# Attention: the second operations of shift and quotient stand behind the next maxima and free the shared PSUM bank themselves

## The chip, the cores and the metric

The kernel runs on one core of one Trainium2 chip. The time is the device time of that core in microseconds (us); several executions are timed, and one more is recorded by the hardware profiler. Engines: PE (TensorE, matmul), PEld (its weight loads, which overlap PE), DVE (VectorE), ACT (ScalarE), POOL (GpSimd), SP (SyncE, which only issues DMAs here).

## What is computed

A stack of eleven steps on x of 16 sequences x 512 tokens x 128 features: attention, recurrent feed-forward, Mamba, feed-forward, latent attention (MLA), mixture of experts, rotary attention, mixture of experts, with layer norms between. The change is in attention, which is used three times with 16 heads of 8 features:

```python
scores = jnp.einsum('bhqd,bhkd->bhqk', q, k) / jnp.sqrt(jnp.float32(D_K))
scores = scores + rel_bias.transpose(2, 0, 1)[None]          # first attention only
scores = jnp.where(causal[None, None], scores, -jnp.inf)     # first and third
attn = jax.nn.softmax(scores, axis=-1)
out = jnp.einsum('bhqk,bhkd->bhqd', attn, v)
out = out.transpose(0, 2, 1, 3).reshape(b, t, d)
return out @ WO.T + bO
```

## The kernel before

`attend` (line 1065) is called three times: with a relative bias and causal (called L0 here), not causal (MLA), and causal with a mask (ROT). A *group* is four heads of one sequence: 4 groups a sequence, 64 groups a call. Each engine has its own hand-written instruction stream, and the streams meet only through semaphores.

The scores are computed twice. `scores_s` (line 1245) puts queries on the partitions, so that DVE (`maxima`, line 1433) can find each query's maximum along the free axis. `scores_t` (line 1272) puts keys on the partitions for exp on ACT (line 1412) and the product with V (`pv`, line 1308, accumulated in `o_ps`). The maxima of a group are turned by PE (`mt`, line 1325), negated and split into a high and a low bf16 part by DVE (`shifts`, line 1465: two operations, the second reads the first's result), stored to DRAM and loaded back by SP as two more rows of the queries (`store_m` line 1182, `load_t` line 1165). The scores run three groups ahead (`AHEAD`).

A group is a step of NTILE tiles for each of two pairs of heads: 3 tiles a pair in the causal calls, numbered 0 to 5 here, 4 a pair, 0 to 7, in MLA. In each tile PE does scores_t of group g, scores_s of group g + 3 and a piece of `pv` of group g - 1. Both kinds of scores go through rings of three PSUM banks (`t_ps`, `s_ps`), two banks a tile, so PE may start scores_s of a tile when DVE has read the second head of the tile before last and the first head of the last tile. In L0 the tiles 0 and 3 get their bias on DVE (`add_bias`, line 1452, line 1460), and the bank of scores_t is free when that is done.

The last PSUM bank, `misc`, is shared by four small uses, in a fixed order; each takes the bank when `misc_read` has counted the use before. They stand behind the tile that `misc_at` names, in PE's stream and in DVE's:

- MT: `mt` on PE, then `shifts` on DVE;
- OT: `ot` on PE (line 1333) turns the group's output, then `divide` on DVE (line 1479) takes the reciprocal of the sums and multiplies;
- BT, once in four groups: `bt` on PE (line 1340), `gather` on DVE (line 1492);
- WO, once in four groups: `wo` on PE (line 1347), `add` on DVE (line 1496) adds the result into x.

In `shifts` and `divide` the second operation follows the first at once behind a wait for it, and a third wait, for the second operation, stands before a sequencer instruction that counts `misc_read` up (lines 1477 and 1490). Inside `maxima` the causal calls count a semaphore `s_seen` before their operations; MLA does not.

Of the kernel before, what the change touches and what calls it, by code (L numbers as in the profile page):

```python
# [25 lines left out]
NB = 16  # L26
# [1038 lines left out]
def attend(core, x, stacks, v_dram, shift_dram, w, scale, causal, bias=None):  # L1065
# [13 lines left out]
    if causal:  # L1079
        tiles = [[(0, 512, 0, 0)], [(0, 384, 1, 128)], [(0, 256, 2, 256), (256, 128, 3, 384)]]  # L1080
        s_tiles = [[(0, 512, 3)], [(0, 128, 0), (128, 384, 2)], [(0, 256, 1)]]
        pv_pieces = [None, (0, 0, 256), (0, 256, 512), (1, 128, 512), (2, 256, 512), (3, 384, 512)]
        misc_at = dict(MT=1, OT=2, WO=4, BT=5)
    else:
        tiles = [[(0, T, k, 0)] for k in range(4)]
        s_tiles = [[(0, T, c)] for c in range(4)]
        pv_pieces = [None, (0, 0, 512)] + [(c, at, at + 256) for c in range(1, 4) for at in (0, 256)]
        misc_at = dict(MT=1, OT=3, WO=5, BT=7)
# [13 lines left out]
    with core.phase() as ph:  # L1102
# [31 lines left out]
        divided = ph.sem("divided")  # L1134
# [18 lines left out]
        def _(sp):  # L1153
# [28 lines left out]
            def store_m(b, k):  # L1182
                bb, g = spread(b, k)
                sp.wait_ge(shift_ready, 2 * (4 * bb + g) + 2)
                sp.dma_start(shift_dram[ds(bb, 1), 4 * g:4 * g + 4].rearrange("a h c r t -> (a h c) r t"),
                             shift[:, g % 2]).then_inc(m_stored[g % 2], 16)
# [6 lines left out]
            store_m(0, 0)  # L1193
            store_m(0, 1)
# [3 lines left out]
            def step(b, g):  # L1198
                n = 4 * b + g
                sp.wait_ge(s_mm, 2 * NTILE * (n + 2) + 2 * NTILE)  # L1200
                load_s(b, g + 4)
                if not (isinstance(b, int) and n == 0):
                    sp.wait_ge(t_mm, USES_OF_GROUP * n)
                sp.wait_ge(v_ready, n + 1 + 1)
                load_t(b, g + 1)
                store_m(b, g + 2)
# [34 lines left out]
        def _(pe):  # L1241
# [98 lines left out]
            def bt(no, b):  # L1340
                use(no)
                pe.wait_ge(divided, 2 * (4 * b + 3) + 2)
# [14 lines left out]
            def step(b, v, g):  # L1357
                started = 4 * b + g if isinstance(b, int) else 99
                for pair, i in itertools.product(range(2), range(NTILE)):
# [11 lines left out]
                    if at == misc_at["BT"] and g == 1 and started >= 4:  # L1371
                        bt(use_no(b, g, "BT"), b - 1)
# [13 lines left out]
            bt(last + 2, NB - 1)  # L1386
# [43 lines left out]
        def _(dve):  # L1430
# [34 lines left out]
            def shifts(no, b, k):  # L1465
# [4 lines left out]
                if not (isinstance(n, int) and n < 2):  # L1470
                    dve.wait_ge(m_stored[g % 2], 16 * (2 * bb + g // 2))
                dve.tensor_scalar(shift[:, g % 2, 0], misc[0:16, 0:P], -1.0, None, ALU.mult).then_inc(shift_ready, 1)
                dve.wait_ge(shift_ready, 2 * n + 1)
                dve.scalar_tensor_tensor(shift[:, g % 2, 1], misc[0:16, 0:P], -1.0, shift[:, g % 2, 0],
                                         ALU.mult, ALU.subtract).then_inc(shift_ready, 1)
                dve.wait_ge(shift_ready, 2 * n + 2)
                dve.sem_inc(misc_read, 1)

            def divide(no, b, k):

                n, g = 4 * b + k, k % 4
# [19 lines left out]
            for k in range(3):  # L1501
                for pair, i in itertools.product(range(2), range(NTILE)):
                    maxima(0, 0, k, pair, i)
                if k:
                    shifts(k - 1, 0, k - 1)

            def step(b, v, g):
                started = 4 * b + g if isinstance(b, int) else 99
                for pair, i in itertools.product(range(2), range(NTILE)):
# [20 lines left out]
            divide(last, NB - 1, 2)  # L1530
            divide(last + 1, NB - 1, 3)
# [835 lines left out]
```

## Time and profile before

| | |
|---|---|
| median of three timed runs | 5572.13 us (5568.46 to 5575.24) |
| profiled execution, own time | 5531.82 us |
| its span | 5529.6 us |
| mean granted TensorE clock | 0.904 |
| busy: PE, DVE, ACT, POOL | 4268.0, 3617.1, 2857.4, 1613.7 us |
| `attend` L0, MLA, ROT in steady flow, us from the span's start | 240 to 1019, 2860 to 3590, 4370 to 4978 |

A busy time is the sum of an engine's operations; semaphore, register and DMA-issuing instructions are not in it. In a row of the timeline the number in brackets at the end is the idle time of that engine just before the instruction, with the one that released it. Small tiles overlap a little, so start to next start is shorter than the duration. The releaser is inferred: where two conditions end close together, the name can be that of either.

### The profile page before, as it was taken

How to read it: one execution, taken by the hardware profiler on the slowest of the kernel's cores; microseconds unless marked ns; L12 is line 12 of the kernel's file. 1: busy time of each engine (PE TensorE's matmuls, PEld its weight loads, DVE VectorE, ACT ScalarE, POOL GpSimd, SP SyncE). 2: the span in 40 equal slices, each digit the busy share in tenths (PEclk: the TensorE clock that was granted, in tenths of full speed). 3: DMA queues.
4: the chain of work that ended last, by engine and by line, in shares of the span. 5: the costliest groups of instructions: out<-in, count | busy, mean ns of one | idle time of the engine just before them, and what ended most of it. 6: DMA issues, size and time to landing. Idle time of an engine off the chain costs nothing. (4 is left out here: it accounts for less than half of the span.)

```text
span 5529.6 us, 110801 instructions
## 1 busy us (share of the span) xinstructions
PE 4268.0 (77%) x31637; PEld 2118.3 (38%) x31638; DVE 3617.1 (65%) x8801; ACT 2857.4 (52%) x5331; POOL 1613.7 (29%) x1559
## 2 busy tenths in 40 slices
PE   6499999987576766778868889853987588885498
PEld 3144444542122222226312222233973233333397
DVE  2488888546699999984279999950115688885012
ACT  7255555664455555556547777731323366663132
POOL 3000000010577777751200000055534100005552
PEclk9699999997799999999669999976998799997699
DMA  7522222003200000000532222213654333331366
GB/s 246 145 76 70 69 75 70 25 22 137 89 25 25 25 25 28 33 13 2 186 96 74 71 77 72 76 52 114 212 176 156 123 92 91 92 90 54 123 212 191
DMA packets 546189, 501.98 MB, mean 91 GB/s; under 512 B 163774, under 2 KB 482911, under 8 KB 545788
## 3 DMA queue, kind: packets, MB, share of 16 engines
q1 hardware_dynamic: 527724, 460.95, 28.0%
q0 software_dynamic: 18160, 37.42, 2.0%
q8 instruction: 135, 2.21, 0.2%
q14 instruction: 170, 1.39, 0.1%
HBM read 330.57 MB, written 167.58 MB: 90 GB/s over the span
## 5 line engine op out<-in xcount | busy, mean ns | idle before, releaser
L1412 ACT ACTIVATE p_probs<-p_t_ps 128x512 f32<-128x512 f32 (+1 forms) x2304 | 1141.8, 551 | 716.6 <-PE p_t_ps L1303 274.8
L1933 PE MATMUL p_y_ps<-p_prod,c_ident 128*128 128x512 f32 x1024 | 550.1, 663 | 307.8 <-DVE p_prod L2116 306.9
L1316 PE MATMUL p_o_ps<-p_probs,p_v_st 128*32 128x256 f32 (+3 forms) x8704 | 726.7, 407 | 2.9 <-ACT p_o_sb L1398 2.9
L2065 POOL TENSOR_TENSOR p_dbx<-p_dtx,p_b_sb 128x512 f32<-128x512 f32 x512 | 642.6, 1279 | 253.2 <-ACT p_b_sb L1964 245.4
L1237 POOL TENSOR_TENSOR p_v_st<-p_v_raw,p_ones 128x128 f32<-128x128 f32 x192 | 87.7, 457 | 2145.8 <-PE p_o_ps L1316 2022.5
L1449 DVE TENSOR_REDUCE p_row_max<-p_s_ps 128x1 f32<-128x512 f32 x1072 | 659.0, 681 | 81.6 <-PE p_s_ps L1254 43.5
L2107 DVE TENSOR_TENSOR_SCAN p_state<-p_da,p_dbx 128x512 f32<-128x512 f32 x512 | 597.7, 1205 | 74.4 <-ACT p_da L2002 54.1
L1285 PE MATMUL p_t_ps<-p_t_q,p_t_k 50*128 50x512 bf16 (+3 forms) x3072 | 516.0, 336 | 164.1 <-ACT p_probs L1412 65.2
L1254 PE MATMUL p_s_ps<-p_s_k,p_s_q 48*128 48x512 bf16 (+3 forms) x3216 | 508.1, 340 | 164.7 <-DMA p_s_k<-stack_k 66.3
L1446 DVE CUSTOM_DVE_ANT_0 p_tried<-p_s_ps,p_s_bias 128x512 bf16<-128x512 f32 (+3 forms) x1072 | 471.5, 487 | 120.2 <-PE p_s_ps L1254 95.8
L1446 DVE CUSTOM_DVE_ANT_0 p_tried<-p_s_ps,c_mask_row 128x512 bf16<-128x512 f32 (+3 forms) x1072 | 469.0, 488 | 104.4 <-PE p_s_ps L1254 49.4
L795 DVE TENSOR_TENSOR p_y<-p_out_ps,p_raw 128x256 f32<-128x256 f32 x142 | 60.3, 424 | 692.7 <-PE p_out_ps L746 692.7
L1933 PEld LDWEIGHTS p_y_ps<-p_prod,c_ident 128*128 128x128 f32 x1024 | 188.7, 202 | 568.0 <-DVE p_prod L2116 489.8
L1285 PEld LDWEIGHTS p_t_ps<-p_t_q,p_t_k 50*128 50x128 bf16 x3072 | 148.9, 93 | 600.8 <-ACT p_probs L1412 343.2
L1964 ACT ACTIVATE p_b_sb<-p_b_ps 128x512 f32<-128x512 f32 x256 | 152.5, 596 | 436.0 <-PE p_b_ps L1902 416.3
L807 POOL DMA_INDIRECT weighed_rows<-p_y,p_raw x284 | 273.2, 962 | 289.3 <-DVE p_y L795 244.8
L2002 ACT ACTIVATE p_da<-p_dt,p_rate 128x512 f32<-128x512 f32 x512 | 334.9, 685 | 29.9 <-DVE p_state L2107 27.9
L777 ACT ACTIVATE p_hidden<-p_hid_ps 128x512 f32<-128x512 f32 x284 | 169.6, 597 | 315.3 <-PE p_hid_ps L735 315.2
L2116 DVE TENSOR_TENSOR p_prod<-p_state,p_c_ps 128x512 f32<-128x512 f32 x512 | 321.7, 668 | 0.0
L1295 PE MATMUL p_t_ps<-p_bias_parts,c_flip 64*128 64x384 bf16 (+2 forms) x4608 | 302.7, 269 | 0.0
L658 POOL DMA_INDIRECT routed_rows<-p_rows,p_index x256 | 252.5, 986 | 121.8 <-issue 73.5
L1412 ACT ACTIVATE p_probs<-p_probs 128x512 f32<-128x512 f32 x256 | 158.4, 628 | 239.2 <-DVE p_probs L1460 239.2
(254 smaller groups left out, 7017.1 us busy)
## 6 DMA issues: line engine op xcount, KB each, us to landing
p_wb<-in_w SPq DMA_DIRECT2D x142, 512.0 KB, 3.7
p_s_q<-stack_q SPq DMA_DIRECT2D x408, 96.0 KB, 2.2
p_s_k<-stack_k SPq DMA_DIRECT2D x408, 96.0 KB, 2.3
p_t_q<-stack_q SPq DMA_DIRECT2D x390, 96.0 KB
p_t_k<-stack_k SPq DMA_DIRECT2D x390, 96.0 KB
mamba_inputs<-p_out SPq DMA_DIRECT2D x17, 1536.0 KB, 5.6
p_inp<-mamba_inputs SPq DMA_DIRECT2D x17, 1536.0 KB, 6.7
stack_q<-p_parts SPq DMA_DIRECT2D x51, 384.0 KB, 2.6
```

Of the source, the lines that this page charges most:

```text
L1254: mm = pe.matmul(s_ps[:, banks[r], at:at + width], s_q[rows, g % 2, pair, c * P:(c + 1) * P], s_k[rows, g % 2, pair, 0:width], start=True, ...
L1285: mm = pe.matmul(out[r], t_k[rows, g % 2, pair, c * P:(c + 1) * P], t_q[rows, g % 2, pair, first:first + width], start=True, stop=not mask ...
L1295: mm = pe.matmul(out[r], bias["flip"][rows, k], bias["t"][q][rows, k, 2 * g + pair, first - c * P:first - c * P + width], start=False, sto ...
L1316: mm = pe.matmul(o_ps[32 * j:32 * j + 32, at:to], v_st[:, g % 2, c, j, :], probs[:, g % 2, j, place[c] + at - first:place[c] + to - first] ...
L1412: act.activation(exps, tile, ACT.Exp, scale=scale).then_inc(expd, 1)
L1446: read = dve.tensor_tensor_reduce(tried[:, slot, at:at + width], scores, over, 1.0, LOWEST, ALU.add, ALU.max, found)
L1449: read = dve.tensor_reduce(found, scores, X, ALU.max)
L1933: pe.matmul(y_ps[:, h], w["ident"], prod[:, k_slot(n, h, RS)], start=(n == 0), stop=(n == STATE - 1)).then_inc(acc_mm, 1)
L2002: act.activation(da[:, k_slot(n, h, RA)], dt[:, u, h], ACT.Exp, scale=rate[:, h, n:n + 1]).then_inc(da_ready, 1)
L2065: pool.tensor_tensor(dbx[:, k_slot(n, h)], dtx[:, u, h], b_sb[:, n % RB], ALU.mult).then_inc(dbx_ready, 1)
L2107: dve.tensor_tensor_scan(out=state[:, out], data0=da[:, k_slot(n, h, RA)], data1=dbx[:, s], initial=0.0, op0=ALU.mult, op1=ALU.add).then_i ...
L2116: dve.tensor_tensor(prod[:, s], state[:, s], c_ps[:, n % 2], ALU.mult).then_inc(prod_ready, 1)
```

## The change

1. `shifts` becomes `shift_high` (behind the maxima of tile MT, as before) and `shift_low` (behind the maxima of the next tile). The low part's operation itself counts `misc_read`; the wait for it and the counting instruction are gone.
2. `divide` is split in the same way: `sums_inverted` behind tile OT, `divide` behind the next one, and the product counts `misc_read`.
3. In the causal calls OT moves from tile 2 to 3 and WO from 4 to 5; in MLA WO moves from 5 to 6. This holds for PE and DVE alike. BT stays.
4. SP's `store_m` waits for `misc_read` of its use, and `bt` drops its own wait for the quotient, since `misc_read` says the same.

```diff
-        misc_at = dict(MT=1, OT=2, WO=4, BT=5)
+        misc_at = dict(MT=1, OT=3, WO=5, BT=5)
...
-        misc_at = dict(MT=1, OT=3, WO=5, BT=7)
+        misc_at = dict(MT=1, OT=3, WO=6, BT=7)
...
-            def store_m(b, k):
+            def store_m(no, b, k):
                 bb, g = spread(b, k)
-                sp.wait_ge(shift_ready, 2 * (4 * bb + g) + 2)
+                sp.wait_ge(misc_read, no + 1)
...
-            def bt(no, b):
+            def bt(no):
                 use(no)
-                pe.wait_ge(divided, 2 * (4 * b + 3) + 2)
...
-            def shifts(no, b, k):
+            def shift_high(no, b, k):
...
                 dve.tensor_scalar(shift[:, g % 2, 0], misc[0:16, 0:P], -1.0, None, ALU.mult).then_inc(shift_ready, 1)
-                dve.wait_ge(shift_ready, 2 * n + 1)
+
+            def shift_low(b, k):
+
+                bb, g = spread(b, k)
+                dve.wait_ge(shift_ready, 4 * bb + g + 1)
                 dve.scalar_tensor_tensor(shift[:, g % 2, 1], misc[0:16, 0:P], -1.0, shift[:, g % 2, 0],
-                                         ALU.mult, ALU.subtract).then_inc(shift_ready, 1)
-                dve.wait_ge(shift_ready, 2 * n + 2)
-                dve.sem_inc(misc_read, 1)
-
-            def divide(no, b, k):
+                                         ALU.mult, ALU.subtract).then_inc(misc_read, 1)
+
+            def sums_inverted(no):
+                dve.wait_ge(misc_mm, no + 1)
+                dve.reciprocal(inv[:, :, :], by_head(misc)[:, :, :, DK]).then_inc(inverted, 1)
+
+            def divide(b, k):
 
                 n, g = 4 * b + k, k % 4
-                view = misc[:, :].rearrange("p (c j d) -> p c j d", c=4, j=4)
-                dve.wait_ge(misc_mm, no + 1)
-                dve.reciprocal(inv[:, :, :], view[:, :, :, DK]).then_inc(divided, 1)
-                dve.wait_ge(divided, 2 * n + 1)
-                dve.tensor_tensor(o_n[:, :, 4 * g:4 * g + 4, :], view[:, :, :, 0:DK],
+                dve.wait_ge(inverted, n + 1)
+                dve.tensor_tensor(o_n[:, :, 4 * g:4 * g + 4, :], by_head(misc)[:, :, :, 0:DK],
                                   inv[:, :, :].unsqueeze(3).to_broadcast([P, 4, 4, DK]), ALU.mult
-                                  ).then_inc(divided, 1)
-                dve.wait_ge(divided, 2 * n + 2)
-                dve.sem_inc(misc_read, 1)
+                                  ).then_inc(misc_read, 1)
...
                     if at == misc_at["MT"]:
-                        shifts(use_no(b, g, "MT"), b, g + 2)
+                        shift_high(use_no(b, g, "MT"), b, g + 2)
+                    if at == misc_at["MT"] + 1:
+                        shift_low(b, g + 2)
                     if at == misc_at["OT"] and started >= 2:
-                        divide(use_no(b, g, "OT"), b, g - 2) if g >= 2 else divide(use_no(b, g, "OT"), b - 1, g + 2)
+                        sums_inverted(use_no(b, g, "OT"))
+                    if at == misc_at["OT"] + 1 and started >= 2:
+                        divide(b, g - 2) if g >= 2 else divide(b - 1, g + 2)
```

## Rows read from the trace of the kernel before

**Rows 1.** Busy time by engine (PE, PEld, DVE, ACT, POOL), clock, DMA: L0, MLA, ROT.

```profile
240.00:1019.00 779.00, 708.64 (x9578) 348.64 (x9578) 690.02 (x2583) 397.94 (x829) 29.36 (x64) 1.00 0.27 72
2860.00:3590.00 730.00, 656.71 (x5732) 190.08 (x5728) 670.41 (x1243) 549.38 (x1031) 27.74 (x61) 0.99 0.27 74
4370.00:4978.00 608.00, 535.79 (x7002) 228.92 (x7000) 526.72 (x2323) 384.14 (x827) 28.74 (x63) 0.99 0.33 91
```

**Rows 2.** Waits of DVE (total us, times, longest) in L0, MLA, ROT.

```profile
DVE p_tried L1446 <- DVE p_shift L1474: 19.6, 52, 0.4
DVE p_probs L1460 <- DVE p_o_n L1486: 13.5, 60, 0.2
...
DVE p_row_max L1449 <- DVE p_shift L1474: 14.7, 57, 0.6
...
DVE p_row_max L1449 <- DVE p_o_n L1486: 13.3, 59, 0.2
...
DVE p_tried L1446 <- DVE p_shift L1474: 25.5, 63, 0.8
DVE p_tried L1446 <- DVE p_o_n L1486: 23.1, 62, 0.4
```

**Rows 3.** Waits of PE, the first row in L0, the second in ROT.

```profile
PE p_t_ps L1285 <- DVE p_probs L1460: 60.3, 127, 0.8
...
PE p_misc L1337 <- DVEq L1477: 21.1, 62, 0.4
```

**Rows 4.** Timeline of one group of ROT: start us, duration us, instruction.

```profile
4597.56 0.69 DVE L1446 CUSTOM_DVE_ANT_0 p_tried<-p_s_ps,c_mask_row 128x512 bf16<-128x512 f32 x1 [0.38 <-PE p_s_ps L1254]
...
4600.29 0.27 DVE L1472 TENSOR_SCALAR p_shift<-p_misc 16x128 bf16<-16x128 f32 x1
...
4600.99 0.66 PE L1337 MATMUL p_misc<-c_ident,p_o_sb 128*128 128x128 f32 x4 [0.32 <-DVEq L1477]
4601.25 0.42 DVE L1446 CUSTOM_DVE_ANT_0 p_tried<-p_s_ps,c_mask_row 128x256 bf16<-128x256 f32 x1 [0.38 <-DVE p_shift L1474]
...
4601.92 0.38 PE L1254 MATMUL p_s_ps<-p_s_k,p_s_q 48*128 48x512 bf16 x2
...
4602.23 0.85 PE L1316 MATMUL p_o_ps<-p_probs,p_v_st 128*32 128x384 f32 x8
4602.23 0.29 DVE L1486 TENSOR_TENSOR p_o_n<-p_misc,p_inv 128x128 f32<-128x128 f32 x1
...
4603.02 0.34 PE L1285 MATMUL p_t_ps<-p_t_q,p_t_k 50*128 50x384 bf16 x2
...
4603.52 0.08 DVE L1446 DVE_READ_ACCUMULATOR2_ANT p_row_max<- 128x1 f32 x1
...
4603.65 0.39 PE L1254 MATMUL p_s_ps<-p_s_k,p_s_q 48*128 48x128 bf16 x4 [0.19 <-DVE p_row_max L1446]
...
4604.24 0.29 DVE L1446 CUSTOM_DVE_ANT_0 p_tried<-p_s_ps,c_mask_row 128x128 bf16<-128x128 f32 x1
...
4605.62 0.42 DVE L1446 CUSTOM_DVE_ANT_0 p_tried<-p_s_ps,c_mask_row 128x256 bf16<-128x256 f32 x1
...
4606.70 0.69 DVE L1446 CUSTOM_DVE_ANT_0 p_tried<-p_s_ps,c_mask_row 128x512 bf16<-128x512 f32 x1 [0.30 <-PE p_s_ps L1254]
```

**Rows 5.** Timeline of L0: bias addition of tile 3, scores_t of tiles 4 and 1.

```profile
612.32 1.29 DVE L1460 TENSOR_TENSOR p_probs<-p_t_ps,xn 128x512 f32<-128x512 f32 x2 [0.22 <-DVE p_o_n L1486]
...
613.07 0.34 PE L1285 MATMUL p_t_ps<-p_t_q,p_t_k 50*128 50x384 bf16 x2 [0.27 <-DVE p_probs L1460]
...
619.40 0.34 PE L1285 MATMUL p_t_ps<-p_t_q,p_t_k 50*128 50x384 bf16 x2 [0.66 <-DVE p_probs L1460]
```

**Rows 6.** Timeline of MLA: scores_s of tile 2, then its maxima.

```profile
3276.46 0.38 PE L1254 MATMUL p_s_ps<-p_s_k,p_s_q 48*128 48x512 bf16 x2
...
3277.18 2.48 DVE L1449 TENSOR_REDUCE p_row_max<-p_s_ps 128x1 f32<-128x512 f32 x4 [0.23 <-DVE p_shift L1474]
```

**Rows 7.** Waits of SP's queue in L0.

```profile
SPq L1162 <- PE p_s_ps L1254: 348.2, 63, 6.7
```

More of the change, by code:

```diff
@@ L1133, in attend @@
         shift_ready = ph.sem("shift_ready")
-        divided = ph.sem("divided")
+        inverted = ph.sem("inverted")
         block = ph.block()
@@ L1192, in _ @@
                 load_s(0, k)
-            store_m(0, 0)
-            store_m(0, 1)
+            store_m(0, 0, 0)
+            store_m(1, 0, 1)
             sp.wait_ge(zeroed, 3)
@@ L1205, in step @@
                 load_t(b, g + 1)
-                store_m(b, g + 2)
+                store_m(use_no(b, g, "MT"), b, g + 2)
             for g in range(4):
@@ L1371, in step @@
                     if at == misc_at["BT"] and g == 1 and started >= 4:
-                        bt(use_no(b, g, "BT"), b - 1)
+                        bt(use_no(b, g, "BT"))
             for g in range(4):
@@ L1385, in _ @@
             ot(last + 1, NB - 1, 3)
-            bt(last + 2, NB - 1)
+            bt(last + 2)
             wo(last + 3)
@@ L1472, in shifts, with by_head @@
                 dve.tensor_scalar(shift[:, g % 2, 0], misc[0:16, 0:P], -1.0, None, ALU.mult).then_inc(shift_ready, 1)
-                dve.wait_ge(shift_ready, 2 * n + 1)
+            def shift_low(b, k):
+                bb, g = spread(b, k)
+                dve.wait_ge(shift_ready, 4 * bb + g + 1)
                 dve.scalar_tensor_tensor(shift[:, g % 2, 1], misc[0:16, 0:P], -1.0, shift[:, g % 2, 0],
-                                         ALU.mult, ALU.subtract).then_inc(shift_ready, 1)
-                dve.wait_ge(shift_ready, 2 * n + 2)
-                dve.sem_inc(misc_read, 1)
-            def divide(no, b, k):
-                n, g = 4 * b + k, k % 4
-                view = misc[:, :].rearrange("p (c j d) -> p c j d", c=4, j=4)
-                dve.wait_ge(misc_mm, no + 1)
-                dve.reciprocal(inv[:, :, :], view[:, :, :, DK]).then_inc(divided, 1)
-                dve.wait_ge(divided, 2 * n + 1)
-                dve.tensor_tensor(o_n[:, :, 4 * g:4 * g + 4, :], view[:, :, :, 0:DK],
+                                         ALU.mult, ALU.subtract).then_inc(misc_read, 1)
[3 more added lines that the diff above has]
+            def divide(b, k):
+                n, g = 4 * b + k, k % 4
+                dve.wait_ge(inverted, n + 1)
+                dve.tensor_tensor(o_n[:, :, 4 * g:4 * g + 4, :], by_head(misc)[:, :, :, 0:DK],
                                   inv[:, :, :].unsqueeze(3).to_broadcast([P, 4, 4, DK]), ALU.mult
-                                  ).then_inc(divided, 1)
-                dve.wait_ge(divided, 2 * n + 2)
-                dve.sem_inc(misc_read, 1)
+                                  ).then_inc(misc_read, 1)
+            def by_head(bank):
+                return bank[:, :].rearrange("p (c j d) -> p c j d", c=4, j=4)
             def gather(no):
@@ L1504, in _ @@
                 if k:
-                    shifts(k - 1, 0, k - 1)
+                    shift_high(k - 1, 0, k - 1)
+                    shift_low(0, k - 1)
             def step(b, v, g):
@@ L1529, in _ @@
             last = use_no(NB, 0, "MT")
-            divide(last, NB - 1, 2)
-            divide(last + 1, NB - 1, 3)
+            for k in (2, 3):
+                sums_inverted(last + k - 2)
+                divide(NB - 1, k)
             gather(last + 2)
```

## The prediction

> **What bounds the kernel now.** The change touches `attend` alone, which runs three times. I read first the busy time of each engine in each attention stage [rows 1]: both PE and DVE are at about 90% in all three (DVE 690 of 779, 670 of 730 and 527 of 608 us; PE 709, 657 and 536), the granted clock is 0.99 to 1.00, and ACT, POOL and the DMA engines have room. So neither engine has a tenth to give; what counts is who waits for whom around the three-bank rings. I call the stages L0 (with the relative bias), MLA (not causal) and ROT (causal with a mask). Each has 16 sequences x 4 groups = 64 groups, so 0.1 us of a group is 6.4 us of the kernel.
>
> Then the waits of DVE in each stage [rows 2]. DVE stands still after its own second shift operation (19.6, 14.7 and 25.5 us) and after its own quotient (13.5, 13.3 and 23.1 us): 109.7 us together, 0.22 us a time where the next step has no counting instruction and nearly 0.4 us where it has one. It is idle that waits for nothing but DVE itself: the operation's completion has to come back before the sequencer may count `misc_read` up and look at the next wait. Last the waits of PE [rows 3]: in L0 60.3 us, twice a group, for `biased` (line 1460), and in ROT 21.1 us, once a group, before the transposes of O (OT, line 1337), for the count at line 1477.
>
> **What the edits do to these waits.** The completion count now comes from the second operation itself, and behind that operation stands no wait on DVE's own work. Between first and second operation a whole maxima tile lies, so that self-wait is satisfied too. The same four operations remain in every group; nothing is added. If all the idle were on the path, 109.7 us would go. It isn't, and I walk one group of each stage to see what is late next.
>
> **ROT** [rows 4]. The group from one tile 0 on DVE to the next is 4597.56 to 4606.70, 9.14 us. With the change, up to the end of the first shift operation nothing differs: 4600.29 + 0.27 + 0.03 - 4597.56 = 3.03. DVE then goes on to tile 2 (before: 0.31 for the second shift operation and 0.38 idle), whose first head takes 0.35 (0.42 less an overlap of 0.07). PE may start scores_s of tile 3 0.13 after that head is read (as 4603.65 follows the head read at 4603.52). From there PE is the late one, since OT now stands behind tile 3's PV piece: scores 0.31 (4601.92 to 4602.23, so 0.07 less than its duration), PV 0.79 (4602.23 to 4603.02), OT 0.59 (0.66 less 0.07), scores_t of tile 4 0.44 (4603.02 to 4603.65, less PE's wait of 0.19), together 2.13. DVE gets tile 4 0.59 after its scores start (4603.65 to 4604.24), takes 1.38 (to 4605.62), then the quotient 0.32 (0.29 at 4602.23 and its gap), then tile 5's first head 0.35, and the next tile 0 comes 0.72 after that (0.13 + 0.59). Sum 3.03 + 0.35 + 0.13 + 2.13 + 0.59 + 1.38 + 0.32 + 0.35 + 0.72 = 9.00 us. So of 0.76 us idle in a group 0.14 us is gained; the rest turns into a wait of DVE for the scores of tile 4: they come 2.13 + 0.59 = 2.72 after those of tile 3 start, while DVE needs 0.59 until it gets tile 3, 1.25 for it and 0.28 for the reciprocal, 2.12, so it stands 0.60. PE's wait of 0.32 before OT (4600.99) goes, as OT comes 1.1 us after the scores of tile 3 while DVE needs 0.35 + 0.28 and a count; it is already in this sum. 64 x 0.14 = **9 us**. Bounds: -0.1 a group (one PE piece 0.3 us longer than I read) to 0.76 (no new wait): -6 to 49 us.
>
> **L0** [rows 5]. PE waits at 613.07 (0.27, scores_t of tile 4, bank held until the bias of tile 3 is added) and at 619.40 (0.66, tile 1). The second one hangs on tile 5's scores, its maxima and then the bias of tile 0: none of that moves, so 0.66 stays. The first one goes: reciprocal, quotient and the idle of 0.22 before the addition at 612.32 now stand behind it or are gone, so the addition comes 0.8 us earlier, and PE, which does the same work in another order, has no pause there. That is 0.27 us, and up to 0.36 if PE's modelled ends hide a little more; I take 0.30. 64 x 0.30 = 19 us. Against it: the addition behind WO now lies between maxima 5 and the bias of the next tile 0, on the path, while before it filled a pause; walked in the same way that costs 0.14 us once in four groups, 2 us. Net **17 us**; bounds 0 (another wait of PE takes the place) to 23.
>
> **MLA** [rows 6]. Scores of tile 2 start at 3276.46 and last 0.38; with 0.04 for the count DVE may read them at 3276.88. DVE ends its first shift operation at 3276.64 (3277.18 less 0.23 idle, 0.28 and 0.03) and would start tile 2 at 3276.88 instead of 3277.18, 0.30 earlier; but the second shift operation, 0.28 and a gap, now follows tile 2: at tile 3 the gain is nil. The shift's idle was hidden by PE's long PV piece ahead of those scores. The quotient's idle is not: before tile 4 the quotient (0.29 + 0.03) and 0.22 idle go, and 0.31 comes back after tile 4. Gain 0.21. 64 x 0.21 = **13 us**; bounds 0 to 0.5 a group (both idles, if the scores of tile 2 come earlier as well), 0 to 32 us.
>
> **The rest, at nothing.** SP: the store of the shifts (line 1185) waits for `misc_read` instead of `shift_ready`, which comes one tile later (0.7 us in the causal stages, 1.2 in MLA). Behind it in SP's queue stands load_s of the next step, and that waits for the scores anyway: 348.2 us in 63 waits in L0, 5.5 each [rows 7]. So the delay is covered; it would take some 5 us to show. BT in a causal stage now follows the quotient of tile 4 closely: PE may wait up to 0.35 us for it once in four groups in ROT, 6 us at most, about made good by WO's move from tile 4 to 5 there; I leave both out. The longer spacing does not touch PE's clock, which is full in all three stages [rows 1]. Prologue and tail: some ten places at 0.1 to 0.3 us, under 3 us, left out.
>
> A rule that speaks against the change: in the trace DVE is idle for 0.22 to 0.38 us behind an operation whose completion it awaits and for about 0.03 us otherwise [rows 2, 4]. The Trainium skill, "VectorE: DVE Perf Modes", section "The DRAIN you can't avoid", says that the pipeline is flushed after each operation whether or not it counts a semaphore, so that counting costs nothing extra, and advises to save operations rather than semaphores. By it the gain would be nothing. It speaks of counting up, though, not of waiting for the count, and the rows of this case differ from it.
>
> **Sum.** 9 + 17 + 13 = 39 us. The profiled execution took 5531.8 us (span 5529.6), so it would take about 5493. The median of the three timed runs is 5572.1, 0.7% above the profiled one; I take the gain off it unscaled: **5533 us**. A measurement of this kernel can tell about 0.2% (11 us) from no change.
>
> **Rivals.** (1) The idle is gained in full: PE keeps up, as it too gets its buffers earlier. For: all 109.7 us are waits for DVE itself, DVE is the busiest engine of MLA. Against: PE is as busy as DVE [rows 1] and has 1.38 us of PV and OT in a row in ROT. It would give 5572 - 105 = about 5467. Chance 0.11. (2) No change within 11 us: what DVE gains, it waits for PE at the next tile, in all three stages; the walk of MLA shows how (0.54 us gone before tile 2, nothing left at tile 3). The rule quoted above, taken as it stands, ends here too: the gap of 0.22 to 0.38 us would remain, behind whatever operation now comes last. 5572. Chance 0.14. (3) Slower: OT behind the long PV piece starves DVE at tile 4. It decides where the scores of tile 4 come more than 0.76 us after DVE is free for them (I get 0.60), or, in L0, where the addition behind WO delays the bias addition. At 0.3 us a group in ROT and 0.15 in L0, 64 x 0.45 = 29 us, less MLA's 13, it gives 5588. For: the only pieces of PE that lie between two scores become 2.13 us where DVE has 1.5 us of work from the moment it gets tile 3. Chance 0.08. The forecast (gains of 15 to 80 us) has 0.67.
>
> **Numbers.** Faster by over 0.2%: 0.67 + 0.11 = 0.78; same 0.14; slower 0.08. The range takes in the forecast case, from 5480 (a gain of 92: most of the three upper bounds 49 + 23 + 32) up to 5576 (no change and its scatter), and leaves out rivals (1) and (3), 0.19.
>
> **What would show it.** In the profile after: no idle on DVE behind the second operations; in its place a wait of DVE for scores before tile 4 in ROT (about 0.6 us a group, 38 us in all) and before tile 2 in MLA (0.24); PE without a wait before OT; PE's wait for `biased` in L0 down from 60.3 to about 43 us; stage lengths shorter by 9 (ROT), 17 (L0) and 13 us (MLA). The prediction is wrong if DVE's idle stays as it is behind the moved operations, if the tile 4 wait exceeds 0.76 us, or if other stages move.

## The result, and the profile after

| kernel | median, us | runs | ratio to before |
|---|---|---|---|
| before | 5570.3 (5556.06 to 5575.24) | 4 | |
| change | 5470.38 (5460.41 to 5478.46) | 4 | 0.983 [0.9803, 0.9857] |

The change is faster by 1.7%. The forecast was 5533 with a range of 5480 to 5576: the direction was right, the size wrong by 63 us, and the range missed the time by 10.

To see where the time came from, I measure each attention stage by one event that both kernels have 64 times: ACT's copy of `o_ps` into `o_sb` (line 1398 before, 1397 after). The rows give the instruction's durations and then the start of its first and its last occurrence; this is ROT, before and then after:

```profile
L1398 ACT ACTIVATE p_o_sb<-p_o_ps x64: 592/592/605, 4388.4 to 4982.2; 128x512 f32<-128x512 f32 x64
```

```profile
L1397 ACT ACTIVATE p_o_sb<-p_o_ps x64: 591/591/603, 4338.5 to 4899.4; 128x512 f32<-128x512 f32 x64
```

| last start less first, us | L0 | MLA | ROT | sum |
|---|---|---|---|---|
| before | 755.7 | 749.9 | 593.8 | 2099.4 |
| after | 736.8 | 720.2 | 560.9 | 2017.9 |
| gained | 18.9 | 29.7 | 32.9 | 81.5 |
| forecast | 17 | 13 | 9 | 39 |

So attention gained 81.5 us: L0 about what was forecast, MLA twice and ROT nearly four times as much. The spans of the two profiles (5529.6 and 5470.2) differ by 59.4 only, because outside attention the profile after took 22 us more. None of it lies in attention, where the change is; the last section says what is known of it.

Busy time by engine (PE, PEld, DVE, ACT, POOL), clock and DMA between those two starts, L0, MLA and ROT, before:

```profile
267.60:1023.30 755.70, 691.21 (x9364) 339.54 (x9360) 669.75 (x2509) 386.63 (x808) 28.00 (x61) 1.00 0.26 71
2855.40:3605.30 749.90, 674.84 (x5912) 196.42 (x5912) 685.23 (x1271) 562.25 (x1056) 27.74 (x61) 0.99 0.27 74
4388.40:4982.20 593.80, 522.49 (x6884) 224.06 (x6884) 513.64 (x2263) 374.63 (x807) 27.83 (x61) 1.00 0.33 91
```

And after:

```profile
265.10:1001.90 736.80, 682.20 (x9364) 348.07 (x9360) 647.42 (x2509) 386.79 (x808) 27.78 (x61) 1.00 0.27 73
2815.00:3535.20 720.20, 666.82 (x5912) 196.41 (x5912) 673.69 (x1271) 562.27 (x1055) 27.74 (x61) 0.99 0.29 77
4338.50:4899.40 560.90, 516.23 (x6884) 227.62 (x6884) 497.50 (x2263) 374.74 (x808) 27.86 (x61) 1.00 0.36 96
```

The windows hold the same instructions (DVE 2509, 1271 and 2263 in both), at the same clock. Yet DVE's *busy* time fell, by 22.3, 11.5 and 16.1 us, 50 together; its idle (length less busy) went from 230.8 to 199.3. In these rows a stretch in which two operations overlap counts once: in ROT the durations alone add up to 637 us before and 633 after, while the busy time is 514 and 498. So 50 us of the 81.5 aren't idle that went, but mostly operations that overlap now and did not before. That is where the size of the forecast failed, and the group below shows it.

The waits changed too. Those of DVE in the steady flow of L0, MLA and ROT (240 to 990, 2825 to 3555, 4300 to 4885; total us, times, longest), where before its own shift and quotient stood [rows 2]:

```profile
DVE p_tried L1445 <- PE p_s_ps L1254: 74.2, 188, 1.1
...
DVE p_row_max L1448 <- PE p_s_ps L1254: 28.2, 67, 4.0
...
DVE p_tried L1445 <- PE p_s_ps L1254: 50.7, 106, 5.7
```

No row of DVE waiting for its own operation is left. In their place DVE waits more for scores: 153 us in all, against 39.0, 14.2 and 20.5 before, 74 together. These windows are not quite those of the table; between the starts of the table, DVE waits 141 us for scores where it waited 68, and 25 us for WO's product (line 1501) where it waited 7. So of 109.7 us of idle some 92 turned into later waits for PE. DVE's idle as a whole fell by 31.5; of that, 14 us are in smaller waits and gaps that I have not taken apart. The wait of PE for the bias in L0 [rows 3], and those of SP's queue in L0 [rows 7]:

```profile
PE p_t_ps L1285 <- DVE p_probs L1459: 52.2, 65, 1.1
...
SPq L1162 <- PE p_s_ps L1254: 252.6, 63, 4.4
SPq L1185 <- DVE p_shift L1477: 86.5, 61, 2.7
```

In L0 PE waits once a group for the bias (65 times) instead of twice (127 times): the wait of `scores_t` of tile 4 is gone. The one of tile 1 grew. Over four groups in a row it was 0.84, 0.65, 0.62 and 0.56 us before (from 509 us on), and is 0.84, 1.03, 0.75 and 0.65 after (from 501 us on). It grew most, by 0.38, where WO's addition now stands in front of the bias addition; there DVE itself waits for WO's product:

```profile
512.03 0.75 DVE L1501 SCALAR_TENSOR_TENSOR x<-p_misc,c_l_b,x 128x512 f32 x1 [0.60 <-PE p_misc L1348]
...
513.44 0.34 PE L1285 MATMUL p_t_ps<-p_t_q,p_t_k 50*128 50x384 bf16 x2 [1.03 <-DVE p_probs L1459]
```

In ROT the wait before OT is gone. There PE waits 0.25 us once in four groups before BT (3.8 us in all), within the 0.35 foreseen, and as much before WO (3.7 us). SP stands 86.5 us for the moved store, and its wait for scores behind it shrinks from 348.2 to 252.6: the delay is covered.

**One group of ROT after**, from one tile 0 on DVE to the next (start us, duration us, instruction, idle ahead and its releaser), to lay beside [rows 4]:

```profile
4527.49 0.69 DVE L1445 CUSTOM_DVE_ANT_0 p_tried<-p_s_ps,c_mask_row 128x512 bf16<-128x512 f32 x1
...
4530.22 0.27 DVE L1471 TENSOR_SCALAR p_shift<-p_misc 16x128 bf16<-16x128 f32 x1
4530.43 0.40 DVE L1445 CUSTOM_DVE_ANT_0 p_tried<-p_s_ps,c_mask_row 128x256 bf16<-128x256 f32 x1
...
4530.89 0.39 PE L1254 MATMUL p_s_ps<-p_s_k,p_s_q 48*128 48x512 bf16 x2
...
4531.99 0.66 PE L1337 MATMUL p_misc<-c_ident,p_o_sb 128*128 128x128 f32 x4
...
4532.59 0.34 PE L1285 MATMUL p_t_ps<-p_t_q,p_t_k 50*128 50x384 bf16 x2
...
4532.87 0.38 PE L1254 MATMUL p_s_ps<-p_s_k,p_s_q 48*128 48x128 bf16 x4
...
4533.45 0.29 DVE L1445 CUSTOM_DVE_ANT_0 p_tried<-p_s_ps,c_mask_row 128x128 bf16<-128x128 f32 x1 [0.49 <-PE p_s_ps L1254]
```

The next tile 0 starts at 4536.10, so the group takes 8.61 us, where it took 9.14 and 9.00 were forecast. The order of events is the one forecast: PE without a pause from scores_s of tile 3 over PV and OT to tile 4, and DVE waiting there, 0.49 us where 0.60 were forecast.

The groups are not all alike. From one `o_sb` to the next ROT takes, over four groups, 9.23, 9.05, 9.79 (with BT) and 10.11 us (with WO) before, and 8.49, 8.45, 9.46 and 9.65 after: 0.74, 0.60, 0.33 and 0.46 less. The forecast's 0.14 was too small in every one of them, and the 0.53 of the group shown is also their mean.

**One group of MLA**, before and then after:

```profile
3265.17 0.28 DVE L1472 TENSOR_SCALAR p_shift<-p_misc 16x128 bf16<-16x128 f32 x1
3265.48 0.28 DVE L1474 SCALAR_TENSOR_TENSOR p_shift<-p_misc,p_shift 16x128 bf16<-16x128 f32 x1
3265.99 2.48 DVE L1449 TENSOR_REDUCE p_row_max<-p_s_ps 128x1 f32<-128x512 f32 x4 [0.22 <-DVE p_shift L1474]
...
3268.39 0.24 DVE L1484 RECIPROCAL p_inv<-p_misc 128x16 f32<-128x16 f32 x1
3268.67 0.29 DVE L1486 TENSOR_TENSOR p_o_n<-p_misc,p_inv 128x128 f32<-128x128 f32 x1
3269.18 7.26 DVE L1449 TENSOR_REDUCE p_row_max<-p_s_ps 128x1 f32<-128x512 f32 x12 [0.22 <-DVE p_o_n L1486]
```

```profile
3208.41 0.28 DVE L1471 TENSOR_SCALAR p_shift<-p_misc 16x128 bf16<-16x128 f32 x1
3208.85 1.29 DVE L1448 TENSOR_REDUCE p_row_max<-p_s_ps 128x1 f32<-128x512 f32 x2 [0.16 <-PE p_s_ps L1254]
3210.06 0.27 DVE L1477 SCALAR_TENSOR_TENSOR p_shift<-p_misc,p_shift 16x128 bf16<-16x128 f32 x1
3210.26 1.26 DVE L1448 TENSOR_REDUCE p_row_max<-p_s_ps 128x1 f32<-128x512 f32 x2
3211.45 0.23 DVE L1482 RECIPROCAL p_inv<-p_misc 128x16 f32<-128x16 f32 x1
3211.73 1.29 DVE L1448 TENSOR_REDUCE p_row_max<-p_s_ps 128x1 f32<-128x512 f32 x2
3212.93 0.28 DVE L1488 TENSOR_TENSOR p_o_n<-p_misc,p_inv 128x128 f32<-128x128 f32 x1
3213.13 6.06 DVE L1448 TENSOR_REDUCE p_row_max<-p_s_ps 128x1 f32<-128x512 f32 x10
```

Read from start to next start, shift and quotient cost DVE 0.82 + 0.79 = 1.61 us a group before, and 0.44 + 0.20 + 0.28 + 0.20 = 1.12 after. The forecast was 1.40.

### The profile page after: what moved, and what is told of

Read it like the earlier page. It is cut to its first block and busy times, and to the rows that moved or that the text cites. A ratio compares the mean times of both kernels' runs of the same rounds, so it can differ in the third digit from the quotient of the medians.

```text
span 5470.2 us, 109878 instructions
## 1 busy us (share of the span) xinstructions
PE 4230.1 (77%) x31637; PEld 2127.4 (39%) x31638; DVE 3565.3 (65%) x8801; ACT 2857.8 (52%) x5331; POOL 1609.7 (29%) x1559
## 5 line engine op out<-in xcount | busy, mean ns | idle before, releaser
L218 PE MATMUL p_var_ps<-p_square,c_mean_mat 128*128 128x512 f32 x256 | 164.1, 727 | 211.6 <-ACT p_square L226 172.8
```

## The experiments

The theory for the size: what was gained comes from DVE's waits for its own operations, and the places do little; my walk undersized it. The rivals: the new places of OT and WO brought the gain, or it is not the wait but the counting instruction that costs. None of the kernels leaves anything out of the computation. "Stages" are lengths as in the table above, L0, MLA, ROT; where a kernel was profiled again they came out within 1 us, MLA within 3.3. The kernel before was profiled once.

| kernel | L0 | MLA | ROT | sum | median, us | before, same chip | ratio |
|---|---|---|---|---|---|---|---|
| change again | 736.8 | 719.9 | 560.7 | 2017.4 | 5422.8 | 5507.1 | 0.9853 [0.9804, 0.9902] |
| count kept | 738.2 | 753.4 | 584.7 | 2076.3 | 5478.54 | 5507.1 | 0.9949 [0.9927, 0.997] |
| count alone | 737.7 | 710.8 | 566.5 | 2015.0 | 5418.26 | 5507.1 | 0.9849 [0.98, 0.9899] |
| places alone | 743.5 | 751.4 | 609.0 | 2103.9 | 5509.66 | 5507.1 | 0.9993 [0.9973, 1.0012] |
| wait kept | 735.4 | 736.6 | 582.2 | 2054.2 | 5455.51, one run | 5507.65 | |
| MT earlier | 724.3 | 711.1 | 565.6 | 2001.0 | 5391.92, one run | 5507.65 | |
| all earlier | 718.3 | 709.9 | 555.8 | 1984.0 | 5380.97, one run | 5507.65 | |
| MLA shift together | 736.8 | 721.3 | 560.8 | 2018.9 | 5426.37 | 5507.65 | 0.9841 [0.9791, 0.9892] |
| early, together | 723.6 | 703.8 | 569.8 | 1997.2 | 5445.69 | 5556.87 | 0.9794 [0.9763, 0.9826] |
| all earlier, timed | 718.5 | 708.1 | 555.9 | 1982.5 | 5428.85 | 5556.87 | 0.976 [0.9727, 0.9794] |
| MLA early, together | 718.3 | 706.8 | 555.8 | 1980.9 | 5443.97 | 5554.6 | 0.9794 [0.9767, 0.982] |
| change, third time | 736.9 | 723.2 | 560.7 | 2020.8 | 5481.4 | 5554.6 | 0.985 [0.9823, 0.9876] |

**The change again**, as made, to stand beside the next three on one chip.

> The change itself, on the chip of the next three kernels. Stage lengths are read from the first to the last move of O (the ACT copy into o_sb) of each attention call: before 755.7, 749.9 and 593.8 us (L0, MLA, ROT), after 736.8, 720.2 and 560.9, so 81.5 us less in attention in one execution each. All theories expect these lengths again within 3 us each. If the 95 us between the medians are attention alone, the lengths must fall by 95; if a stage outside attention scatters (the second routing stage took 21.6 us longer in the one execution of the change), the whole time differs from run to run by more than the attention stages do.

2017.4 against 2017.9: the stages repeat. The median is 84.3 us under the kernel before on the same chip, and attention is 82.0 shorter, so attention accounts for it.

**The count kept.** The moved order, but the second operation is awaited and the sequencer counts, as before.

> The changed kernel with both second operations at their new places, but each followed again by the wait for it and by the sequencer's count of misc_read. Theory A (the gain is DVE's own idle behind the second operations): the idle of 0.22 us (MLA) and nearly 0.4 us (causal) comes back at the new places, twice a group; MLA loses about 0.45 x 64 = 29 us of its 30, ROT and L0 at least 10 each, together 50 to 75 of the 81.5. Rival B (the gain is that PE gets the shared bank sooner and in a better order): only the 0.1 us of the count's way is lost, and attention stays within 15 us of the change. Rival C (the gain is the distance between first and second operation, so that the second one no longer waits): all of it stays.

```diff
-                                         ALU.mult, ALU.subtract).then_inc(misc_read, 1)
+                                         ALU.mult, ALU.subtract).then_inc(second, 1)
+                dve.wait_ge(second, 4 * bb + g + 1)
+                dve.sem_inc(misc_read, 1)
```

(and the same for the product.) It gives back 58.9 of 82 us: 33.5 in MLA, 24.0 in ROT, 1.4 in L0. In sum that is what theory A expects, but not in L0, where at least 10 us should have come back. The idle is back behind the moved operations in MLA:

```profile
3184.50 0.27 DVE L1479 SCALAR_TENSOR_TENSOR p_shift<-p_misc,p_shift 16x128 bf16<-16x128 f32 x1
3185.00 1.29 DVE L1450 TENSOR_REDUCE p_row_max<-p_s_ps 128x1 f32<-128x512 f32 x2 [0.23 <-DVE p_shift L1479]
```

Start to start 0.50 where the change takes 0.20.

**The count alone.** The kernel before in every order and place, but the second operations count `misc_read` themselves; SP's store waits for `misc_read` and BT's own wait is dropped, as in the change.

> The kernel before with one part of the change alone: the second operations count misc_read themselves, nothing stands behind them, and all four operations and OT, WO and BT stay where they were. Theory A: most of the gain is here. MLA 0.45 us a group, 29 us; L0 15 to 20 us; ROT 20 to 33 us; in all 60 to 80 of the 81.5 us. The gap before the second operation, 0.03 us plus the overlap of 0.07 to 0.10 us that neighbours have without a wait, stays lost: 5 to 15 us. Rival C (distance is what counts): less than half, under 40 us. Rival B: PE's wait before OT in ROT shrinks by 0.1 only and the stages gain under 15 us in all.

```diff
                 dve.scalar_tensor_tensor(shift[:, g % 2, 1], misc[0:16, 0:P], -1.0, shift[:, g % 2, 0],
-                                         ALU.mult, ALU.subtract).then_inc(shift_ready, 1)
-                dve.wait_ge(shift_ready, 2 * n + 2)
-                dve.sem_inc(misc_read, 1)
+                                         ALU.mult, ALU.subtract).then_inc(misc_read, 1)
```

84.4 us in attention, as much as the whole change: 2.4 us more in sum, 9.1 better in MLA, 5.8 worse in ROT. Against the kernel before, L0 gains 18.0 and ROT 27.3, both as expected, and MLA 39.1 where 29 were. In MLA both pairs stand together with no idle about them:

```profile
3188.46 0.27 DVE L1471 TENSOR_SCALAR p_shift<-p_misc 16x128 bf16<-16x128 f32 x1
3188.76 0.28 DVE L1473 SCALAR_TENSOR_TENSOR p_shift<-p_misc,p_shift 16x128 bf16<-16x128 f32 x1
3188.98 2.48 DVE L1448 TENSOR_REDUCE p_row_max<-p_s_ps 128x1 f32<-128x512 f32 x4
3191.38 0.25 DVE L1481 RECIPROCAL p_inv<-p_misc 128x16 f32<-128x16 f32 x1
3191.66 0.29 DVE L1483 TENSOR_TENSOR p_o_n<-p_misc,p_inv 128x128 f32<-128x128 f32 x1
3191.87 7.25 DVE L1448 TENSOR_REDUCE p_row_max<-p_s_ps 128x1 f32<-128x512 f32 x12
```

0.52 + 0.49 = 1.01 us a group, against 1.12 in the change and 1.61 before. The second operation, which awaits the first, starts 0.30 and 0.28 us behind it, where one that awaits nothing follows after 0.20: awaiting the operation just issued costs about 0.1 us in this place. So the split into two places was worth nothing in MLA.

**The places alone.** The kernel before with OT at 3 and WO at 5 (6 in MLA).

> The kernel before with OT moved from tile 2 to 3 and WO one tile later, and nothing else: first and second operations together, wait and count as before. Theory A: DVE's idle is all there; MLA unchanged within 2 us, ROT loses PE's wait of 0.32 us before OT but DVE is not faster for it: within 10 us of before; L0 within 10 us. Rival B (the order of PE's work makes the gain): ROT and L0 20 us or more faster.

```diff
-        misc_at = dict(MT=1, OT=2, WO=4, BT=5)
+        misc_at = dict(MT=1, OT=3, WO=5, BT=5)
...
-        misc_at = dict(MT=1, OT=3, WO=5, BT=7)
+        misc_at = dict(MT=1, OT=3, WO=6, BT=7)
```

No gain in sum (4.5 us more in attention, ratio 0.9993): L0 12.2 shorter, ROT 15.2 longer, MLA 1.5 longer. L0 and ROT both moved by more than the 10 us that I had allowed. In ROT the idle behind the shift now delays tile 2, PE stands for its head, and OT behind the late tile 3 delays the next scores, so that both engines stand in turn:

```profile
4567.87 0.42 DVE L1446 CUSTOM_DVE_ANT_0 p_tried<-p_s_ps,c_mask_row 128x256 bf16<-128x256 f32 x1 [0.38 <-DVE p_shift L1474]
...
4568.36 0.39 PE L1254 MATMUL p_s_ps<-p_s_k,p_s_q 48*128 48x512 bf16 x2 [0.64 <-DVE p_row_max L1446]
```

The rival that the places bring the gain falls for the sum, for MLA and for ROT. In L0 it holds in part, and the effects don't add: L0 gains 18.0 by the count alone and 12.2 by the places alone, but 18.9 by both. The traces show that each takes away the same wait. Between the stage's two starts PE waits for the bias 123 times before (58.0 us), and 61 times, once a group, with the count alone (42.9), with the places alone (47.0) and with both (49.9). The wait of `scores_t` of tile 4 is gone in all three.

**The wait kept.** The change, in which DVE waits behind each second operation for its count, with no counting instruction.

> The changed kernel, where each second operation counts misc_read itself, but DVE still waits for that count before it goes on. So PE gets the bank as early as with the change, and DVE has the self-wait but not the sequencer's counting instruction. Theory A (the price is the wait for an own operation): stage lengths close to those with wait and count kept (738.2, 753.4, 584.7), at most 10 us less in all; in MLA at least 740. Rival D (the price is the counting instruction in the sequencer): close to the change (736.8, 719.9, 560.7). Half way, MLA near 735, would mean both.

```diff
                                          ALU.mult, ALU.subtract).then_inc(misc_read, 1)
+                dve.wait_ge(misc_read, no + 1)
```

It gives back 36.8 us: MLA 16.7, ROT 21.5, and L0 1.4 better. In MLA:

```profile
3190.35 0.27 DVE L1477 SCALAR_TENSOR_TENSOR p_shift<-p_misc,p_shift 16x128 bf16<-16x128 f32 x1
3190.74 1.29 DVE L1448 TENSOR_REDUCE p_row_max<-p_s_ps 128x1 f32<-128x512 f32 x2
3191.95 0.25 DVE L1483 RECIPROCAL p_inv<-p_misc 128x16 f32<-128x16 f32 x1
3192.11 1.22 DVE L1448 TENSOR_REDUCE p_row_max<-p_s_ps 128x1 f32<-128x512 f32 x2
```

0.39 us from the start of the second operation to the next tile, against 0.20 without the wait and 0.50 with wait and counting instruction. So in MLA the price has two parts: 0.19 for the wait and 0.11 for the instruction that the sequencer had to issue behind it. The stage says the same (16.7 of 33.5; the expectation had called MLA near 735 the case of both, and it is 736.6). In ROT nearly all that the stage gives back (21.5 of 24.0) is the wait, though DVE's own idle there is 31.8 us with the wait alone and 44.5 with both. Neither cause alone is the answer. In both kernels the reciprocal is 0.16 to 0.17 us ahead of the next tile, where in the change it is 0.28; I don't know why. It gives back 0.12 us a group and is in the stage lengths: 2 x 0.19 - 0.12 = 0.26, times 64 = 17 us, as measured.

**MT one tile earlier**, at 0 in all calls.

> The changed kernel with MT one tile earlier: PE turns the maxima behind tile 0, where no PV piece stands, DVE's first shift operation follows tile 0's maxima and the second one tile 1's. Theory: in ROT and L0 PE waits at tile 1 for ACT or for the bias anyway (28.4 and 52.2 us a stage), so the 0.21 us of this transpose fall into idle time; ROT 5 to 13 us shorter, L0 0 to 10, MLA 5 to 15, as DVE's wait for the scores of tile 2 (0.16 to 0.26 us a group) goes. Rival: PE now waits at MT for the last maxima of the step before (the last head's 0.35 or 0.6 us) and stands there; MLA and ROT 10 us or more longer.

```diff
-        misc_at = dict(MT=1, OT=3, WO=5, BT=5)
+        misc_at = dict(MT=0, OT=3, WO=5, BT=5)
...
-        misc_at = dict(MT=1, OT=3, WO=6, BT=7)
+        misc_at = dict(MT=0, OT=3, WO=6, BT=7)
```

L0 12.5 (0 to 10 expected) and MLA 8.8 us shorter; ROT, which I had expected to be 5 to 13 shorter, 4.9 longer. There PE's wait for ACT nearly went, as expected (27.3 us in the change, 2.9 here), but PE now waits before MT for WO's addition and BT's gather (4.7 and 3.1 us), and DVE waits 58.7 us for scores instead of 40.2. I have not shown which of them makes the stage longer.

**All uses earlier.**

> The changed kernel with every place one earlier: MT 0, OT 2, WO 4, BT 4 in the causal calls and MT 0, OT 2, WO 5, BT 6 in MLA. Against the kernel with MT alone earlier it tells what OT's place is worth once no idle stands behind the operations. Before, moving OT and WO later by one tile cost ROT 15 us and gave L0 12 us. If that comes from PE's order alone, ROT here is about 15 us shorter than with MT alone moved and L0 12 longer. If it came from the idle behind the operations, which stood between the tiles, the two kernels are within 5 us of each other in each stage.

```diff
-        misc_at = dict(MT=1, OT=3, WO=5, BT=5)
+        misc_at = dict(MT=0, OT=2, WO=4, BT=4)
...
-        misc_at = dict(MT=1, OT=3, WO=6, BT=7)
+        misc_at = dict(MT=0, OT=2, WO=5, BT=6)
```

33.4 us below the change in attention: L0 18.5, MLA 10.0, ROT 4.9. Against the run before it, OT's earlier place brought ROT 9.8 (15 expected) and L0 6.0 where I had expected it to cost 12. PE's wait for the bias in L0 shows what was relieved, 23.5 us in 63 waits with MT alone earlier and 25.8 in 63 with all, where the change has 50.4 in 63 (240 to 970 us).

**In MLA the shift together again**, right behind its first operation; the quotient split.

> The changed kernel, but in MLA the two shift operations stand together behind tile 1, the second counting by itself; the quotient stays split, the causal calls as changed. With both pairs together MLA took 710.8 instead of 719.9 us. Theory: the 9 us are DVE's wait for the scores of tile 2 (0.16 to 0.26 us a group), which the second shift operation fills when it stands there; so MLA comes to 711 to 713, L0 and ROT stay at 736.8 and 560.7, attention 9 us below the change, whole time 0.1 to 0.2% below it. Rival: the 9 us come from the quotient together; MLA stays at 718 to 720.

```diff
-                    if at == misc_at["MT"] + 1:
+                    if at == misc_at["MT"] + (1 if causal else 0):
```

I had put down MLA's 9 us to the shift's split alone. It fell: 721.3, no better than the change. The shift now takes 0.52 instead of 0.64 us, but the tile 4 that follows the reciprocal isn't there yet:

```profile
3213.36 0.26 DVE L1471 TENSOR_SCALAR p_shift<-p_misc 16x128 bf16<-16x128 f32 x1
3213.66 0.28 DVE L1477 SCALAR_TENSOR_TENSOR p_shift<-p_misc,p_shift 16x128 bf16<-16x128 f32 x1
3213.88 2.48 DVE L1448 TENSOR_REDUCE p_row_max<-p_s_ps 128x1 f32<-128x512 f32 x4
3216.28 0.25 DVE L1482 RECIPROCAL p_inv<-p_misc 128x16 f32<-128x16 f32 x1
3216.76 1.29 DVE L1448 TENSOR_REDUCE p_row_max<-p_s_ps 128x1 f32<-128x512 f32 x2 [0.23 <-PE p_s_ps L1254]
```

What is gained at the shift is waited for at tile 4. With both pairs together, the quotient's second operation fills that wait (3191.38 to 3191.87 above).

**Early and together.** The count alone, with the places of the version with all uses earlier.

> Both pairs of operations together, the second one counting misc_read itself (no wait and no counting instruction behind it), at the earlier places: MT 0, OT 2, WO 4, BT 4 in the causal calls, MT 0, OT 2, WO 5, BT 6 in MLA. Against the same places with the pairs split (718.3, 709.9, 555.8) it tells what the split itself is worth. Theory: next to nothing, as the split at the old places was worth 0.9 us in L0, 5.8 in ROT (there together with OT's move) and minus 9 in MLA; each stage within 6 us of the split kernel. Rival (the distance between the operations is worth the 0.1 us of overlap twice a group): 12 us longer in each stage.

```diff
-        misc_at = dict(MT=1, OT=2, WO=4, BT=5)
+        misc_at = dict(MT=0, OT=2, WO=4, BT=4)
...
-        misc_at = dict(MT=1, OT=3, WO=5, BT=7)
+        misc_at = dict(MT=0, OT=2, WO=5, BT=6)
```

**All uses earlier, timed**, the same kernel as above, beside it on the same chip.

> The kernel with all places one earlier and the pairs split, again, now timed in rounds. Stage lengths 718, 710 and 556 us again; its whole time 115 us (2.1%) below the kernel before and 33 us (0.6%) below the change, outside the scatter of the other stages.

Together it takes 1997.2, split 1982.5: at these places the split is worth 5.1 us in L0 and 13.9 in ROT, and costs 4.3 in MLA. I had expected a difference within 6 us: right in L0 and MLA, missed in ROT. What the split saves in ROT shows as a wait of PE in the version without it, which the other does not have:

```profile
PE p_s_ps L1254 <- DVE p_row_max L1445: 21.2, 57, 0.4
```

I read it so: the second operation right behind the first delays the head that scores wait for; behind the next maxima it doesn't.

**All uses earlier, in MLA both pairs together**, and **the change a third time**, on one chip.

> The same as the run with every place earlier for the causal heads (second operations behind the next maxima, places one row tile earlier), but in the MLA heads both pairs stand together, each second operation right behind its first, which counts the read. By stages it should be the best of both: L0 718.4, MLA 703.8 (what the run with all pairs together took there), ROT 555.8, sum 1978 us, 4 to 5 us below the run with every place earlier and 39 us below the change as made. Rival: the MLA stage depends on what the stages around it leave behind, and comes out at 708 to 710, so that splitting or not makes no difference there; sum 1983.

> The changed kernel again, to stand on the same chip beside the version with the earliest places: stages 736.8, 720.0, 560.8 and sum 2018, as in its earlier profiles, and 82 us below the kernel before in attention. If the version with the earliest places gains by the stages alone, the two medians differ by 39 us; the rival is that they differ by less than 30 because the stages outside attention take it back.

MLA comes out at 706.8, between the two expectations (703.8 and 708 to 710), and the change's own MLA at 723.2, against 720.2 and 719.9, shows a scatter of 3.3 us; whether the pairs should stand together in MLA stays open. The medians differ by 37.4 us where 39.9 are expected from the stages, so what the earlier places gain, nothing takes back. The best version is the one with all uses earlier, in either form: ratios 0.976 and 0.9794 against the change's 0.985, and on the one chip where both ran, the intervals [0.9767, 0.982] and [0.9823, 0.9876] don't meet.

## Why the prediction was right in direction and wrong in size

**The mechanism held in the main.** Nearly all that was to show did, in its place: no idle on DVE behind its own operations, a wait for scores before tile 4 in ROT (0.49 us, 0.60 forecast) and before tile 2 in MLA (0.16, 0.24 forecast), no wait before OT, PE's wait for the bias in L0 once a group. Its size there is not the forecast one: 52.2 us for 43.

**L0: the number right, in part by luck.** It gained 18.9 for 17. The wait of tile 4 went, as forecast. But "0.66 stays" was wrong: the wait of tile 1 grew by 0.15 us a group, some 9 us in the stage. Most of that is in the group with WO's addition: 0.38 us there, where I had 0.14. So PE's idle fell by 9.9 us, not by 17. The other 9.0 us are busy time of PE that overlaps now. I had allowed 0.03 us a group for that, and it is 0.14. The two errors made up for each other.

**ROT, 0.39 us a group mis-sized.** Measured by the terms of the forecast's sum: up to the end of the first shift operation 2.94 (forecast 3.03); to scores_s of tile 3 0.46 (0.48); from there to scores_s of tile 4 1.98 (2.13); to DVE's tile 4 0.58 (0.59); tile 4 1.38 (1.38); the quotient 0.21 (0.32); the rest 1.06 (1.07). Sum 8.61 against 9.00. The three terms that failed are two kinds:

- The small operations of DVE, "0.27 + 0.03" and "0.32": I took a duration and a gap, as they stand in the row before, where something waits behind them [rows 4]. Without a wait a small operation overlaps its neighbour: 4530.22 to 4530.43 is 0.21 us for an operation of 0.27. That is 0.20 us a group.
- "scores_t of tile 4 0.44 (4603.02 to 4603.65, less PE's wait of 0.19)": without a wait it is 0.28 (4532.59 to 4532.87), so PE had waited 0.35 there, not 0.19. The bracket of a matmul counts from the modelled end of the one before, and that end comes after the next matmul's start even where nothing waits (4532.59 + 0.34 is 4532.93). That is 0.16 us a group.

Both errors have one sign: durations and brackets understate what an engine gains when a wait goes. The 50 us less of busy DVE are the first of them: 0.18 us a group in MLA (11.5 over 64), most of which is the two second operations, each followed after 0.20 us and not after its 0.28, and 0.35 and 0.25 in L0 and ROT, where more operations overlap than I have taken apart.

**MLA, 0.28 us a group.** Of 1.61 us the forecast left 0.51 for the first shift operation, 0.31 for the second, 0.28 for the reciprocal and 0.31 for the product, together 1.41 (1.40 by its gain of 0.21); measured 0.44, 0.20, 0.28 and 0.20. The two operations behind the maxima were priced at 0.31, though nothing waits behind them: 0.22. The remaining 0.07 is tile 2, whose scores came earlier than I read.

Put together: ROT 0.53 us a group times 64 = 34 (stage 32.9), MLA 0.49 times 64 = 31 (29.7), L0 18.9.

**Of the 63 us** between forecast and result, 42.5 are attention's, as above (81.5 less 39). Some 19 more are the part of the 100 us between the two medians that is not attention's, and the change did not make it. With attention's 81.5 alone the time would have been 5489, inside the range. So the sizes were wrong, and it was the part outside attention that put the time below 5480.

**The parts at nothing.** SP's store and the clock were at nothing. BT cost PE 3.8 us of waiting in ROT. WO's move was not the help that I took it for: in ROT PE waits 3.7 us before WO and DVE 9.6 us for its product, and in L0 DVE waits 9.0, where none of these waits stood before. What they cost the stage was not measured.

**The rivals.** (1) All idle gained: fell, though its time of 5467 is next to the measured 5470. That is luck. DVE's idle fell by 31.5 of the 109.7 us, the other 50 are overlap, and 19 are not attention's. (Its sum takes off 105, where the idle is 109.7.) By the runs on single chips the gain was 84 and 73 us. (2) No change: fell. The walk of MLA behind it, where nothing is left at tile 3, was wrong by the mis-sized second operation. The rule of the Trainium skill, "VectorE: DVE Perf Modes", section "The DRAIN you can't avoid", that counting costs nothing extra, is not contradicted: an operation that counts `misc_read` is followed after 0.20 us, but no run here leaves the count out. The runs show what the rule does not speak of: waiting for that count costs 0.19 us in MLA, and a counting instruction behind it 0.11. The page's advice to save operations rather than semaphores, which stands in its section "Rules for kernel authors", fails here: the same four operations remain, and 84.4 us went. (3) Slower: fell; PE's 1.98 us between the scores of tiles 3 and 4 left DVE 0.49 idle, under the 0.76 from which it decides.

**What I had not asked** is which part brings the gain. The count by the second operation itself, two lines fewer at each place, brings 84.4 us alone. The split costs MLA 4.3 us at the earlier places and pays 13.9 in ROT there. At the change's places it was not tried by itself: split and places together cost MLA 9 us and pay 5.8 in ROT. The places chosen in the change brought nothing alone and were not the best for it.

## What to carry to other kernels

Let the last operation count the semaphore by which a shared buffer comes free, in place of a wait for it and a counting instruction, and only then ask where it should stand. Size a wait that goes by start-to-start distances of the same operations where nothing waits behind them, not by durations and brackets. Once a wait is gone, try the places again: here one tile earlier was worth 33 to 35 us more.

## What the runs showed of the hardware

- Behind a DVE operation of 0.27 to 0.28 us with no wait the next one starts 0.20 to 0.21 us after it did. A wait for the operation just issued makes it 0.39, and a counting instruction behind that wait 0.50 (MLA).
- The time outside attention has two levels with the same instructions. From the last `o_sb` of MLA to the first of ROT it is 777 to 786 us in the profile before and in the first eight experiments, and 802 to 807 in the profile after and in the last four; the tail has 544 to 550 and 570 to 573. The kernel before ran at 5507 us on the two chips of the first level and at 5555 and 5557 on the two of the second. The routing stage shows it: the weights of the first expert are loaded (first start in each row, before and then after) 216.3 us after MLA's last `o_sb` in the one and 238.9 in the other.

```profile
L735 PEld LDWEIGHTS p_hid_ps<-p_xt,p_wb x1136: 190/190/337, 3821.6 to 5458.8; 128*128 128x128 f32 x190
```

```profile
L735 PEld LDWEIGHTS p_hid_ps<-p_xt,p_wb x1136: 190/190/338, 3774.1 to 5397.9; 128*128 128x128 f32 x190
```

The profile before (5531.8 us) was of the first level. Its timed runs, by their times, were of the second, which would explain the 40 us between them. On each of the four chips of the experiments only one level was seen; why, these runs don't show.
- A third stretch scatters by itself: from L0's last `o_sb` to MLA's first it is 1797 to 1844 us in the fourteen profiles, with the same instructions. The granted clock there is 0.90 where it is 1800 and 0.88 where it is 1844. It was 1832.1 in the profile before and 1813.1 in the one after. So the 22 us that the profile after took more outside attention are 20.2 and 23.4 of the two stretches above, less 19.0 of this one and 2.5 before L0's first `o_sb`.

A gain of 40 us is safe only where both kernels ran on one chip, or where the stage is measured by itself.
